# A gated delta-net layer with an FP4 feed-forward on one core: the device loop over sequences replaced by straight-line code

## What is computed

```python
xn = _layernorm(x, axis=-1)
x = x + gated_delta_net(xn, ...) + fp4_ffn(xn, w_gate, w_up, w_down)
# gated_delta_net, 12 heads, DK = 64, DV = 128, one step per token:
#   q, k, v = silu(causal 4-tap convolution of xn @ Wq, Wk, Wv); q, k L2-normed
#   S = S * exp(g_t);  delta = (v_t - k_t S) * beta_t
#   S = S + k_t (x) delta;  o_t = q_t S
#   out = (rmsnorm(o) * gnorm * silu(xn @ Wg)) @ Wo
# fp4_ffn: x, weights and the hidden layer rounded to FP4 in blocks of 16
```

## Time and profile before

| | us |
|---|---|
| median of 3 executions | 2946.46 |
| lowest, highest | 2942.95, 2953.33 |
| span of the profiled execution, first to last instruction | 2943.5 |
| VectorE, ScalarE, GpSimd busy in it | 2423.7, 2295.6, 1635.3 |
| TensorE matmul busy in it | 2669.1 |
| TensorE clock, mean granted | 0.977 of full |

### The profile page before, as it was taken

One profiled execution on the slowest core, in us unless ns is written; L12 is line 12 of the kernel. 1 busy time (PEld: TensorE's weight loads), 2 busy tenths in 40 slices (PEclk: granted clock), 3 DMA queues, 4 the chain that ended last, 5 costly groups with the idle time before them and its releaser, 6 DMA issues.

```text
span 2943.5 us, 84345 instructions
## 1 busy us (share of the span) xinstructions
PE 2669.1 (91%) x25584; PEld 2100.7 (71%) x25679; DVE 2423.7 (82%) x6817; ACT 2295.6 (78%) x7010; POOL 1635.3 (56%) x2418
## 2 busy tenths in 40 slices
PE   5899999999999998999999999999999999999997
PEld 3577777777777777777777777777777777777776
DVE  7888888888788888888888888888888878888872
ACT  4688787878788887887877878887888878788874
POOL 3566555566545666455655555665456664556651
PEclk8899999999999999999999999999999999999997
DMA  2111011111111111111110111111111101111101
GB/s 68 27 31 34 16 35 37 36 28 30 22 35 37 27 36 25 24 37 37 26 37 14 35 37 31 32 27 25 35 37 26 37 21 29 37 32 31 34 14 23
DMA packets 319420, 91.28 MB, mean 31 GB/s; under 512 B 283056, under 2 KB 310000, under 8 KB 318960
## 3 DMA queue, kind: packets, MB, share of 16 engines
q1 hardware_dynamic: 318960, 85.59, 14.0%
HBM read 46.76 MB, written 38.80 MB: 29 GB/s over the span
## 4 chain that ended last, share of the span: by engine, by line
PE 47%; DVE 19%; issue 13%; POOL 9%; ACT 5%; DMA 3%; SPq 1%; DVEq 1%; POOLq 1%; ACTq 0%
DVE UP L1015 6%; PE ring L1393 4%; PE ring L1236 4%; POOL laneA L614 4%; POOL laneT L611 4%; DVE KQ L918 4%; PE ring L1177 4%; PE bank_o L1357 3%; PE ring L1186 3%; PE bank_e L1339 2%; PE bank_e L1326 2%; PE bank_e L1343 2%; PE ring L1376 2%; PE bank_o L1369 2%; PE ring L1219 2%
## 5 line engine op out<-in xcount | busy, mean ns | idle before, releaser
L611 POOL TENSOR_TENSOR laneT<-laneA 96x30 f32<-96x30 f32 (+14 forms) x960 | 518.0, 540 | 68.0
L614 POOL TENSOR_TENSOR laneA<-laneA,laneT 96x30 f32<-96x30 f32 (+14 forms) x960 | 512.6, 534 | 75.3
L918 DVE SCALAR_TENSOR_TENSOR KQ<-ring,ckq,KQ 128x255 f32<-128x255 f32 (+2 forms) x1152 | 459.8, 473 | 14.7 <-DVE nabs L953 6.3
L918 DVE SCALAR_TENSOR_TENSOR vc<-ring,cvv,vc 128x255 f32<-128x255 f32 (+2 forms) x1152 | 462.3, 472 | 0.3
L1060 DVE SCALAR_TENSOR_TENSOR V<-bank_o,eG,V 128x128 f32<-128x128 f32 x384 | 133.5, 348 | 285.1 <-PE bank_o L1363 233.9
L1015 DVE SCALAR_TENSOR_TENSOR UP<-ring,cj,gm 128x256 f32<-128x256 f32 x768 | 315.3, 476 | 27.2 <-PE ring L1203 19.3
L598 POOL TENSOR_TENSOR sqk<-sse,phalf 128x8 f32<-128x8 f32 x96 | 157.4, 1640 | 306.7 <-DVE sse L989 306.7
L592 POOL TENSOR_TENSOR gm<-g,mle 128x512 f32<-128x512 f32 x192 | 197.6, 1052 | 169.5 <-DVE UP L1015 161.0
L782 ACT ACTIVATE eps<-bank_e 128x128 f32<-128x128 f32 x384 | 106.4, 277 | 229.4 <-PE bank_e L1343 186.5
L606 POOL MEMSET laneA<- 96x32 f32 x32 | 4.9, 154 | 480.8 <-DMA laneA<-to_lanes 480.8
L625 POOL TENSOR_TENSOR rO<-ov,mhalf 128x8 f32<-128x8 f32 x96 | 166.4, 1734 | 155.4 <-DVE ov L1071 155.1
(11 more groups left out here) (161 smaller groups left out, 7926.0 us busy)
## 6 DMA issues: line engine op xcount, KB each, us to landing
to_lanes<-UP SPq DMA_DIRECT2D x128, 96.0 KB, 2.7
laneA<-to_lanes SPq DMA_DIRECT2D x32, 384.0 KB, 3.1
from_lanes<-laneA SPq DMA_DIRECT2D x32, 384.0 KB, 3.2
UP<-from_lanes SPq DMA_DIRECT2D x128, 96.0 KB, 3.1
turned_lanes<-laneX SPq DMA_DIRECT2D x32, 288.0 KB
N<-turned_lanes SPq DMA_DIRECT2D x96, 96.0 KB, 2.7
xin<-_attn_hidden_states_dram SPq DMA_DIRECT2D x32, 128.0 KB, 3.2
xres<-_attn_hidden_states_dram SPq DMA_DIRECT2D x32, 128.0 KB, 2.2
```

Of the source, the lines that this page charges most:

```text
L611: link(nc.gpsimd.tensor_tensor(t, A[:, 0:m, j:j + 1].broadcast_to([LANES, m, n]), A[:, j:j + 1, j + 1:BLK].broadcast_to([LANES, m, n]), AL ...
L614: link(nc.gpsimd.tensor_tensor(w, w, t, ALU.add))
L918: ins = nc.vector.scalar_tensor_tensor(acc[:, n, s:T], src[:, n * T:n * T + T - s], wt(n)[:, TAPS - 1 - s:TAPS - s], acc[:, n, s:T], ALU.m ...
```

## The change

Three things are done, on all five engines. `run` calls `iteration` from Python for all 34 iterations, so there is no loop on the engines. Every wait thereby compares with a constant, since the iteration number is a Python integer everywhere. `hold` and `split` and all their calls are deleted, with the semaphore `held`. Which waits there are, on which semaphores and for which counts, the steps, their order and the data they move stay as they are.

```diff
-        s_held = sem("held")
-        def hold(eng):
-            eng.sem_inc(s_held, 1)
-        def split(eng, *sems):
-            if len(set(id(s) for s in sems)) < len(sems):
-                hold(eng)
...
         def run(eng, iteration):
-            for it in range(-2, 4):
-                parity[0] = it % 2
-                iteration(it)
-            with eng.Fori(4, NB - 3, 2) as it:
-                for n in range(2):
-                    parity[0] = n
-                    iteration(it + n)
-            for it in (NB - 2, NB - 1):
+            for it in range(-2, NB):
                 parity[0] = it % 2
                 iteration(it)
...
                         if not zero(i):
-                            hold(sp)
                             sp.wait_ge(s_xcd, i * 16 * TURNED)
...
                             pool.wait_ge(s_lin, cnt(i, 1, 1) * 16)
-                            hold(pool)
...
                                 pool.wait_ge(s_tout, i * 16)
-                                hold(pool)
...
                             link(nc.vector.bn_stats(stats[:, t, :], xin[:, t, :]))
-                            hold(dve)
                             link(nc.vector.bn_aggr(mv[:, t, :], stats[:, t, :]))
...
                         b = take("MZ", a)
-                        split(pe, read("MZ", a), read("MY", a))
                         pe.wait_ge(read("MY", a), rv(i, "MY", a))
                         if a == 0:
                             pe.wait_ge(s_xc, cnt(i, 1, 1) * 16 * NBL)
-                        hold(pe)
```

More of the change, by code:

```diff
@@ L676, in iteration @@
                         if not early(i):
-                            split(act, full("XN", 0), full("GP", 5))
                             act.wait_ge(full("GP", 5), rv(i - 2, "GP", 5))
@@ L682, in iteration @@
                         act.wait_ge(s_z, cnt(i, 1, 1))
-                        hold(act)
                         nc.scalar.preload_act_table_set("natural_log_exp_and_others")
@@ L717, in iteration @@
                             for t in range(NT):
-                                split(act, full("VP", a), *(full("VT", a - a % 2 + n) for n in range(t + 1)))
                                 act.wait_ge(full("VT", a - a % 2 + t), rv(i - 1, "VT", a - a % 2 + t))
@@ L734, in iteration @@
                         if not early(i):
-                            split(act, full("OT", a), full("VT", a))
                             act.wait_ge(full("OT", a), rv(i - 2, "OT", a))
@@ L769, in iteration @@
                         if a or not zero(i):
-                            split(act, full(*use), full(*before))
                             act.wait_ge(full(*before), rv(i if a else i - 1, *before))
@@ L1160, in iteration @@
                         b = take("ZB", 0)
-                        split(pe, read("ZB", 0), read("XN", 0))
                         pe.wait_ge(read("XN", 0), rv(i, "XN", 0))
@@ L1182, in iteration @@
                         if a == 0:
-                            split(pe, read("QK", 0), read("XN", 0))
                             pe.wait_ge(read("XN", 0), rv(i, "XN", 0))
@@ L1246, in iteration @@
                         for j in range(2):
-                            split(pe, read("XQ", 0), read("FU", a, j))
                             b = take("FU", a, j)
@@ L1284, in iteration @@
                         b = take("MY2", a)
-                        split(pe, read("MY2", a), read("MZ", a))
                         pe.wait_ge(read("MZ", a), rv(i, "MZ", a))
-                        hold(pe)
                         for n in range(GU):
@@ L1293, in iteration @@
                         y, z = take("MX", a, 0), take("MX", a, 1)
-                        split(pe, read("MX", a, 1), read("MZ", a))
                         pe.wait_ge(read("MZ", a), rv(i, "MZ", a))
-                        split(pe, read("MZ", a), read(*y2(a - 1)))
                         pe.wait_ge(read(*y2(a - 1)), rv(i, *y2(a - 1)))
-                        hold(pe)
                         for n in range(GU):
@@ L1305, in iteration @@
                         b = take("MZ2", a)
-                        split(pe, read("MZ2", a), read(*y2(a)))
                         pe.wait_ge(read(*y2(a)), rv(i, *y2(a)))
-                        hold(pe)
                         for n in range(GU):
@@ L1323, in iteration @@
                                     ready = z2(h // GH)
-                                    split(pe, read("VT", h // 2), read(*ready))
                                     pe.wait_ge(read(*ready), rv(i, *ready))
@@ L1331, in iteration @@
                                     pe.wait_ge(read("KT", 0), rv(i, "KT", 0))
-                                    split(pe, read("KT", 0), read("KT", 1))
                                     pe.wait_ge(read("KT", 1), rv(i, "KT", 1))
@@ L1372, in iteration @@
                         t, q = a % 2, a // 2
-                        split(pe, read("OT", a), read("GP", a))
                         pe.wait_ge(read("GP", a), rv(i, "GP", a))
```

2 lines of the change are left out of this document (removed).

## The result

The changed kernel took 2871.66 us (median of 4 runs, 2869.09 to 2873.21), the kernel before 2947.9 in the runs beside it: ratio 0.974, interval 0.9726 to 0.9753. That is 76 us less where 65 were forecast (2882), inside the range of 2863 to 2902. The profiled execution has a span of 2871.5 us.

What follows compares the result with a forecast made beforehand. TensorE's stream with short waits, plus what the loop adds, was taken as the bound. From the 2943.5 us span, 29, 27, 6 and 3 came off, giving 2879, or 2882 as measured; range 2863 to 2902.

Steps and rivals of the forecast that it cites:

- 12 back edges: Taken branches at the loop's end: 2.4 us each (90.8 against 88.4 per iteration), clock drops included, 29 us saved.
- register arithmetic: ALU instructions computing wait values inside the loop: 1.0 us per iteration over 26 iterations, 27 us saved.
- increments: No-effect semaphore increments on all five engines: 0.2 us per iteration over 32 iterations, 6 us saved.
- rarer collisions: Code packets meeting the lane chain's fetch less often than in the first three straight iterations: 3 us saved.
- The view: Times of L1091, which ends each iteration on VectorE: 87.37 us written out, 89.52 in the loop, 56 us over 26 iterations.
- the straight iterations: Iterations -2 to 3 and 30, 31, already outside the loop with the same steps; 1 to 3 took 87.37 us each.
- signs named: Profile after: L1091 every 87 us or less without alternation, L375 and ALU instructions gone, clock 1.00, chain waits 0 to 1 us.
- the lane chain: Stores and loads through DRAM around POOL's 45 us elimination, second partner ahead of MY; claimed to be late next.
- Rival 1: Only the back edges count, register instructions run hidden beside running work: 2917 us, chance 0.08.
- The prediction's sum by that price: With a compare-and-branch at about 108 ns, 12 taken branches are worth 1.3 us; result near 2917.
- Rival 2: All iterations run at straight iteration 2's 86.9 us and increments bring 0.4 each: 2866 us, chance 0.12.
- Rival 3: Slower: lane chain bounds every iteration, TensorE stops ahead of MY, clock drops, 2.4 us per iteration: 2960 us, chance 0.02.

Runs made afterwards that it cites:

- experiment 1: Kernel before with the loop written out from Python, all waits constant, but every no-effect semaphore increment kept: 2884.24 us, ratio 0.9788.
- experiment 2: Kernel before with loop bodies of 12 iterations (two trips, one taken back edge), the rest written out: 2906.54 us, ratio 0.9863.
- experiment 3: Kernel before with loop bodies of 4 iterations (six trips, five taken back edges), the rest written out: 2926.76 us, ratio 0.9926.
- experiment 4: Kernel of experiment 1 with only TensorE's increments kept, those of the other engines removed: 2869.21 us, ratio 0.973.
- experiment 9: The changed kernel run again unaltered, as the measure for the runs beside it: 2866.11 us, ratio 0.974.
- experiment 11: Kernel of experiment 1 with only VectorE's three increments per iteration kept: 2877.39 us, ratio 0.9769.
- experiment 12: Changed kernel with SP's fetch of the plain blocks (for MZ) moved ahead of that of the turned ones (for MY): 2908.29 us, ratio 0.9881.

## Why the prediction was right, and where its terms were off

| term | forecast | measured | by |
|---|---|---|---|
| 12 back edges | 29 | about 44 | 62.7 less the registers (experiments 1 to 3) |
| register arithmetic | 27 | 16 to 19 | 26 x 0.62 to 0.72; with 16, the loop's entry has 2.4 |
| increments | 6 | 11 to 15 | experiments 1, 4, 9 and 11 |
| rarer collisions | 3 | not seen | see below |
| sum | 65 | 76 | |

**The view was the right one.** The step list was the same inside the loop and outside it, the straight iterations gave the pace, and most of the time came from what the loop adds to them. Reading L1091 alone gave 56 of the 62.7 us of the loop. Most signs named came: no L375, no ALU instructions, no stop before QK of a back edge's size, waits of up to 1.1 us for the lane chain. Two did not: the granted clock fell once in the straight code, in iteration 3, and some iterations do alternate, by 0.9 us, with the waits ahead of MZ.

**The edge was undersized, the registers oversized.** The step that failed is "an iteration that follows a back edge takes 90.8, one that does not 88.4, so an edge is worth 2.4". It took the 88.4 iterations as free of what a trip's start costs. They were its tail, with a wait of 0.6 to 1.4 us ahead of MZ for the plain blocks: experiments 2 and 3 give 5.05 where the tail may run out, and 3.7 in the kernel before, where it may not. The same error put the difference of 1.0 us to the straight code wholly on the registers, where 0.6 to 0.7 belongs to them. The two errors have opposite signs and mostly cancel, 56 against 62.7; that the sum came out this near is in part luck. That iterations 4 and 5, ahead of any edge, also took 88.45 is what made the reading persuasive. But they stand at the loop's entry, and in experiment 2 the entry's iterations are slow too, 88.2 against 87.6 for those further in. Rival 1, that only the edges count, is refuted by the 15 to 17 us that remain between experiments 1 and 2 when the edge, and the entry, are taken off. The 108 ns for a compare-and-branch that the Trainium skill, page "Advanced Engine Details and Errata", section "Control Flow Timing", gives are not what a taken edge cost here, 3.7 us. The prediction's sum by that price is wrong as well: 2946.5 - 1.3 - 27 - 6 - 3 = 2909, not 2917.

**The increments: right in sign, wrong in place.** I gave them 0.2 us per iteration "since most of them stand in the matrix steps MY to MZ2" and costed those on VectorE at nothing because "TensorE's products cover them". TensorE's cost nothing, and VectorE's three cost 0.7 in an undisturbed iteration. At the iteration's beginning VectorE isn't covered: TensorE waits for its cumulative sum ahead of L1136, as it did in the kernel before. And I priced them by their own duration, 21 ns, while two of them put 0.11 each between dependent instructions and the shift put another one in POOL's way. In the kernel before `nabs` (L953) took 504 ns in the median, 178 at least; this was there to be read.

**What was late next.** The text said the lane chain would be, and it is. It explains much of why 0.7 us in an undisturbed iteration become only 11.3 / 32 = 0.35 on average: the faster kernel waits longer for the plain blocks. The longest rows of these waits, experiment 9 first, then 11:

```profile
PE ring L1239 <- DMA UP<-from_lanes: 5.1, 9, 1.1
...
PE ring L1273 <- issue: 2.0, 4, 0.8
```

Over all products of step MZ they are 10.4 and 4.6 us, 5.8 of the 11 us given back; ahead of MY they are alike, 1.2 and 1.3 beside the last iteration. Two iterations of experiment 9, of 88.8 and 88.5 us with the clock at half for a stretch, are some 4 us more. For the collisions I expected a gain of 3 us, since code packets would meet the fetch more rarely. They did: its three issues took over 2 us in 5 of 30 iterations of the changed kernel (2.04 to 2.90), one in six, where it had been two of the first three straight ones (2.14 and 2.51). But the gain is not seen, since the one in iteration 3 cost more than before: a drop of the clock came with it, 90.9 against 87.5.

**The rivals.** Rival 2 had 2866 from 86.9 in all iterations and 0.4 for the increments; the result lies between it and the forecast, and nearer to it (5.7 and 10 us). Both its halves were nearer than mine: with the increments in, the straight iterations took 87.02 on average, and 15 us over 32 iterations are 0.47. It had been given a chance of 0.12. Rival 3, the slower one, did occur in one iteration, and experiment 12 shows what it would have been in all: 88.08, still less than the 89.52 of the kernel before. Its price, 2.4, was too high, as the stop was 1.2 us on average and the clock did not fall in every iteration.

## What to carry to other kernels

When a loop's cost is read from iterations with and without a back edge, ask how long the iterations behind the start of a trip stay slow, and what they wait for: in a short body no iteration is free of it, the loop's entry is not free of it either, and a longer body is the experiment that tells (12 iterations instead of 2 gave 40 of the 63 us here). Instructions without effect are to be priced by what stands between two dependent instructions on the engine that others wait for, not by their number: sixteen on TensorE cost nothing measurable, three on VectorE 11 us. And when the engines get faster, look at the just-in-time transfer ahead of the next step; its margin decides how much of a gain is given back.

## What the runs showed of the hardware that was not expected

- A semaphore increment between two dependent VectorE instructions adds 0.11 us from start to start (0.32 to 0.43), five times its own 21 ns.
- A VectorE instruction on 24 elements takes 0.18 us alone and 0.55 when a POOL instruction of 0.57 us has begun just ahead of it, in the one-operand and the two-operand form alike. Not every one is held: `sp`, of the same size, took 0.17 with a start 0.04 behind one of POOL's. Why the shift by about 0.1 us makes the two meet in most iterations of one kernel and in none of the other is not settled, nor whether the length of `nabs` alone makes the 0.39.
- A stop of TensorE of 1.0 us was followed by 0.71 and 0.78 of the clock over twenty microseconds in iteration 3, while a back edge of the kernel before passed at 1.00. Behind the other edges but one of that kernel, ten of twelve, a stretch was at 0.50 to 0.52 (627.0 to 633.8 us: 0.50); and in the changed kernel a stop of 1.1 us ahead of step MZ passed at 1.00. The length of the stop alone doesn't tell the two apart.
- An edge of the loop costs 5.05 us in all, of which some 2 fall in the three iterations behind it, as waits for the lane chain; the loop's entry, where no branch is taken, costs 2.4 us in the same way.
